# Moving the second chunk's state products, y and their VectorE steps behind the FFN work of their slot

## The reference, cut to what matters

```python
def step(h, inp):
    x_c, dt_c, B_c, C_c = inp
    lcs = jnp.cumsum(dt_c * A, axis=1)
    ...
    M = jnp.exp(jnp.where(mask, diff, -jnp.inf))
    G = jnp.einsum('blhn,bihn->bhli', C_c, B_c)
    intra = jnp.einsum('bhli,bihp->blhp', M * G, x_c)
    inter = jnp.einsum('blh,blhn,bhpn->blhp', jnp.exp(lcs), C_c, h)
    total_decay = jnp.exp(lcsT[:, :, -1])
    h_new = total_decay[:, :, None, None] * h + jnp.einsum('bhl,blhp,blhn->bhpn', M[:, :, -1, :], x_c, B_c)
    return (h_new, intra + inter)
...
y = y + x_h * D[None, None, :, None]
y = y * jax.nn.silu(z)
y = rmsnorm(y, w_norm_out)
...
sh = jax.nn.relu(jnp.einsum('bsd,ndf->bsnf', x, sw1) + sb1)
shared = (jnp.einsum('bsnf,nfo->bsno', sh, sw2) + sb2).sum(axis=2) / NS
rh = jax.nn.relu(jnp.einsum('bsd,edf->bsef', x, rw1) + rb1)
eo = jnp.einsum('bsef,efo->bseo', rh, rw2) + rb2
routed = (top two experts of four, weighted)
```

## Time and profile before

| | us |
|---|---|
| median of 3 runs | 567.0 (566.67 to 570.47) |
| profiled execution, its own time | 565.39 |
| span of its trace | 563.7 |

### The profile page before, as it was taken

One profiled execution on the slowest core, in us unless ns is written; L12 is line 12 of the kernel. 1 busy time (PEld: TensorE's weight loads), 2 busy tenths in 40 slices (PEclk: granted clock), 3 DMA queues, 4 the chain that ended last, 5 costly groups with the idle time before them and its releaser, 6 DMA issues.

```text
span 563.7 us, 11668 instructions
## 1 busy us (share of the span) xinstructions
PE 542.6 (96%) x3912; PEld 428.5 (76%) x3912; DVE 443.3 (79%) x1044; ACT 352.3 (63%) x760; POOL 173.2 (31%) x232
## 2 busy tenths in 40 slices
PE   8887989999999999999999999999999999999996
PEld 7665767878777777877787777778777787877774
DVE  5887878978889787878888788887888788775654
ACT  4894578637775478736786387745786377752442
POOL 3083505521162203620155201722045211532010
PEclk9998999999999999999999999999999999999999
DMA  7650017200570007500371005500162004600130
GB/s 207 196 141 9 1 55 182 74 1 1 160 169 1 2 6 218 107 1 0 100 192 34 0 0 165 160 0 0 39 208 78 0 0 142 169 1 1 32 68 19
DMA packets 37353, 41.41 MB, mean 73 GB/s; under 512 B 3482, under 2 KB 27716, under 8 KB 37316
## 3 DMA queue, kind: packets, MB, share of 16 engines
q1 hardware_dynamic: 36724, 40.80, 26.0%
q10 hardware_dynamic: 592, 0.15, 0.1%
HBM read 37.79 MB, written 3.15 MB: 73 GB/s over the span
## 4 chain that ended last, share of the span: by engine, by line
PE 59%; DVE 21%; ACT 8%; issue 7%; DMA 2%; POOL 2%; DVEq 0%; ACTq 0%; SPq 0%; POOLq 0%
PE bank L426 9%; PE bank L428 6%; PE bank L427 6%; PE bank L536 6%; PE bank L641 5%; PE bank L642 5%; PE bank L643 5%; DVE cv L1124 5%; DVE act_l L1275 4%; PE bank L548 3%; ACT act_h L873 3%; PE bank L564 2%; PE bank L522 2%; DVE dsum L1140 2%; DVE dtv L1138 2%
## 5 line engine op out<-in xcount | busy, mean ns | idle before, releaser
L1275 DVE SCALAR_TENSOR_TENSOR act_l<-bank,act_h 128x512 fp32r<-128x512 f32 x192 | 131.7, 687 | 51.5 <-ACT act_h L873 49.9
L873 ACT ACTIVATE act_h<-bank 128x512 fp32r<-128x512 f32 x192 | 114.7, 597 | 81.9 <-PE bank L428 78.1
L1501 POOL TENSOR_TENSOR late<-late 128x512 f32<-128x512 f32 x31 | 39.8, 1285 | 166.9 <-DVE late L1283 166.9
L426 PE MATMUL bank<-fTl,w1h 128*128 128x512 f32 x192 | 87.0, 453 | 2.0 <-DVE act_l L1275 0.7
L893 ACT ACTIVATE seg<-seg,lneg 128x128 f32<-128x128 f32 x256 | 81.3, 395 | 0.0
L641 PE MATMUL bank<-act_l,w2h 128*128 128x512 f32 x192 | 77.6, 404 | 1.5 <-DVE act_l L1275 1.5
L642 PE MATMUL bank<-act_h,w2l 128*128 128x512 f32 x192 | 76.0, 396 | 0.0
L428 PE MATMUL bank<-fTh,w1h 128*128 128x512 f32 x192 | 75.7, 394 | 0.0
L427 PE MATMUL bank<-fTh,w1l 128*128 128x512 f32 x192 | 75.5, 393 | 0.0
L643 PE MATMUL bank<-act_h,w2h 128*128 128x512 f32 x192 | 75.5, 393 | 0.0
L1488 POOL TENSOR_TENSOR xw<-xs,seg 128x128 f32<-128x128 f32 x48 | 20.2, 421 | 147.0 <-ACT seg L893 69.8
(11 more groups left out here) (177 smaller groups left out, 1057.9 us busy)
## 6 DMA issues: line engine op xcount, KB each, us to landing
seg<-lc_rows SPq DMA_DIRECT2D x32, 512.0 KB, 3.8
late<-gk_rows SPq DMA_DIRECT2D x8, 1024.0 KB, 9.0
grow<-lc_rows SPq DMA_DIRECT2D x48, 128.0 KB, 4.9
x_in<-L_attn_hidden_dram SPq DMA_DIRECT2D x8, 256.0 KB, 2.8
out_dram<-late SPq DMA_DIRECT2D x8, 256.0 KB, 5.3
late<-L_ffn_sw_dram SPq DMA_DIRECT2D x2, 512.0 KB, 6.3
late<-L_ffn_rw_dram SPq DMA_DIRECT2D x1, 1024.0 KB, 7.1
CT<-L_attn_w_in_proj_dram SPq DMA_DIRECT2D x1, 512.0 KB, 5.3
```

The source lines that it names most:

```text
L426: mm(dst, stat_h, mov_l, start=True, stop=False)
L873: nc.scalar.activation(act_h[:, b % RING, :], HID[b % 2][:], ACT.Relu).then_inc(act_h_ready, 1)
L1275: v_.scalar_tensor_tensor(act_l[:, r, :], HID[b % 2][:], 0.0, f(act_h[:, r, :]), ALU.max, ALU.subtract)\
```

## The change

Nothing is computed differently. For the passes with a scan and an FFN, `y_product` of chunk 1 is taken from the front of slot 17 and put behind `first` and `second` of that slot; VectorE's step 2 of chunk 1 is taken from the front of the slot and put behind `routed_out` and `act_low`. The opening keeps its order.

```diff
@@ TensorE, scan_part and body
                     if step == 2:
-                        y_product(s, c)
+                        if c != 1:
+                            y_product(s, c)
...
                     if old := block_at(i - LAG, prev, older):
                         second(*old)
+                    if s is not None and i == CHUNKS_FROM + 5:
+                        y_product(s, 1)
@@ VectorE, scan_part and body
-                if i >= CHUNKS_FROM:
+                if i >= CHUNKS_FROM and (i != CHUNKS_FROM + 5 or is_seq(s, 0)):
                     attend(s, *divmod(i - CHUNKS_FROM, 3))
...
                     if (new := block_at(i, prev, older)) and not (i == 0 and prev is not None):
                         act_low(*new)
+                    if s is not None and i == CHUNKS_FROM + 5:
+                        attend(s, 1, 2)
```

## The result

The changed kernel takes **573.86 us** (median of 4 runs, 571.09 to 575.33), the kernel before 566.84 beside it: a ratio of 1.0121, with a 95% interval of 1.0092 to 1.015. A second set of runs gave 574.01 against 566.40, ratio 1.0149 (1.0108 to 1.0189). It is slower by more than 1%, 0.5 us from the forecast of 573.4.

What follows compares the result with a forecast made beforehand. TensorE, busy 96% of the span, was taken as the bound. 5.2 us (sequences 1 to 6) plus 1.2 (sequence 7) gave 6.4 on the profiled 565.39, so 571.8; with the median 1.6 higher, 573.4. Range 566.8 to 577.0.

Steps and rivals of the forecast that it cites:

- Steps 1 to 3: Slots 17 and 18: FFN products start earlier, `y_product` and GpSimd's work later; `state_m` is 2.3 us late.
- Step 4: VectorE's `state_m` collides with GpSimd's first decay mask, is stretched and ends 0.27 us behind it.
- the other bound: Alternative in step 4: `state_m` unstretched at 0.41 to 0.42 us, all that follows 0.16 us earlier.
- Steps 5 and 6: Silu(z) product meets `CTe`, `hn` waits for `late`; chunk 2's `mg` 1.38 us late, TensorE stands 0.86 longer, 5.2 in all.
- Step 7: Chunk 3's growth rows are issued late, ScalarE waits 2.1 us; costs TensorE 1.2 us, in sequence 7 only.
- I take nothing: Step 7's late growth rows cost nothing in sequences 1 to 6, where TensorE is itself 0.86 us late.
- (a): Rival: `hn` gets the ports ahead of `late`, TensorE keeps 0.23 us per pass: 565.4 to 567, chance 0.17.
- (b): Rival: growth rows land later and decide in every sequence, 1.65 us more each, 11.6 in all: 585, chance 0.10.
- (c): Rival: the change does nothing measurable, losses of steps 6 and 7 lie in unseen waits: 567, chance 0.03.

Runs made afterwards that it cites:

- the added GpSimd instruction: Changed kernel plus one useless 128x512 TENSOR_TENSOR on GpSimd right behind the first `late` of a pass: 584.13 us, ratio 1.0333.
- the kernel with both edits: Changed kernel with `hn` at the front of slot 17 and a third growth-row buffer: 566.27 us, ratio 0.9984; again 566.51, ratio 1.0000.
- the third buffer: Growth rows of chunks 1, 2 and 3 in buffers of their own; as the only edit to the changed kernel: 572.33 us, ratio 1.0096.
- the kernel before with both edits: Kernel before, in its old order, with `hn` ahead of `routed_out` at the end of slot 17 and a third growth-row buffer: 576.68 us, ratio 1.0186.
- the kernel with VectorE's order alone: Only VectorE's part of the change, against the kernel before; `y_product` stays ahead of the FFN products: 589.87 us, ratio 1.0421.

## Why the prediction was right, step by step

**Steps 1 to 3** came out. Against the last product of `second(11)`, `y_product` starts 0.23 later (0.23 predicted), `routed_out` 0.69 (0.59), `state_m` 1.95 (1.85), GpSimd's first mask 1.67 (1.68) and `late` 4.66 (4.68). The 0.10 of `routed_out` is new: it waited for a DMA. More of that below.

**Step 4**, `state_m` under the mask: right in sequences 4 to 6, 0.58 to 0.72 us with the end 0.28 behind the mask (0.27 predicted). In sequence 3 it came later still, behind a longer wait for the DMA, and took 0.50 under the `xw` behind the mask. In sequences 1, 2 and 7 the order of the two was the other one. VectorE and GpSimd in sequence 1:

```profile
102.58 0.41 DVE L1171 TENSOR_TENSOR state_m<-state,grow 128x256 f32<-128x256 f32 x1
...
104.66 3.05 DVE L1103 TENSOR_SCALAR hn<-x_in,mv,rs 128x128 f32<-128x128 f32 x4
```

```profile
102.62 0.88 POOL L1497 TENSOR_SCALAR_AFFINE_SELECT seg<-seg 128x508 f32<-128x508 f32 x1
```

`state_m` began 0.04 ahead of the mask, took 0.41, and the mask was the one stretched, 0.88 for 0.64. So the one that starts first goes through, in both directions. The Trainium skill's page "SBUF — State Buffer" has it so in its section "Who interferes with whom", and this trace agrees, with the 0.41 and the 0.88. Which of them is first hangs here on 0.1 us of `routed_out`. The prediction had taken the 0.41 of the other bound for an absence of contention. It also misread its 16 rows: none stood beside a mask, but the first one (0.41 us from 38.52) ran wholly inside a GpSimd TENSOR_TENSOR of 128x8 (line 1430, 37.48 to 39.13) and was not stretched, so not every pair of this sort collides. The silu(z) product then came ahead of `CTe`, but `hn` behind it met `CTe` and `late` both and took 3.05. Chunk 2's weights came 0.82 later than before there too; the 0.16 that the other bound would have saved were not saved.

**Steps 5 and 6** carry the forecast, and hold: chunk 2's weights 0.81 later in sequence 5 against 0.86, and 0.80 to 0.85 in all of sequences 1 to 6. The first experiment that takes `late` from `hn` and the one that takes `hn` from `late` both remove this wait, and the added GpSimd instruction lengthens it by what it adds to `hn`. The six passes together lost 4.3 us, not 5.2, so this term was over-sized by 0.9: chunk 2 was 0.82 late on the mean of six instead of 0.86, and by chunk 3 another 0.07 to 0.08 was made up each time (7.66 us from chunk 2's weights to chunk 3's where it was 7.74; the kernel with both edits, where TensorE doesn't wait, has 7.75). Why the products behind a wait stand closer I did not look into.

**Step 7** had the right place and a size that varies. It gave 1.2 us to sequence 7; measured were 0.5 and 2.2 in two traces. The step that failed is the transfer left out of it. `routed_out` multiplies by the gating rows, a load of 1 MB for which it did not have to wait at its old place: in sequence 5 before, the load landed at 360.37 and `routed_out` started at 362.27. The change moves it 2 us ahead, into the landing (364.26, with `routed_out` at 364.29): waits in slot 17 of sequences 3 to 6, of 0.9 to 1.5 us, where there was none, and in five passes of the second trace, with 2.35 in its sequence 7. There the load landed 10.26 us behind its issue where it had been 8.60. No run moved this load, so its share is read from the traces alone. The prediction followed the growth rows, which are issued later, and not the rows that are needed sooner.

"I take nothing" for the growth rows in sequences 1 to 6 held, but only since TensorE was late already. With `hn` out of the way chunk 3's weights came up to 0.7 us later than before in a pass, and with the third buffer besides that was gone. Had the first term been smaller, this one would have come up in its place.

**The sum**: 6.4 us predicted. The two pairs of traces, from the opening's end, show 4.6 and 6.8, the medians 7.0 and 7.6. It is right within 0.5 us by cancelling: the passes' term was 0.9 too large, and what the medians hold beyond the traces stands in no term. Both traced executions of the changed kernel were the fastest of their sets (571.09 and 572.13), and 2 to 3 us lie between them and the medians. Part of it may be half-clock stretches: 5 of the 10 runs have a mean granted clock of 0.990 to 0.992 where the traced ones have 0.995. But one run with 0.995 took 578.86, so that isn't all; a later landing of the gating rows would do it too. No trace caught either, and the cause of these 2 to 3 us stays open.

**The rivals.** (a), `hn` ahead of `late`, did not occur in any of the twelve passes: GpSimd's waiting instruction went first each time. What it would have given is nearest to the two kernels that keep `hn` and `late` apart: 1.009 times the time of before, and no gain, since the growth rows then decide. The gain that (a) counted on shows only with these out of the way too: 0.2 us in most passes of the traces, as predicted, and nothing in the medians. (b) fell by its condition, as above. (c) fell.

## What to carry to other kernels

When instructions of one engine are moved, list for every instruction in the moved block both what it frees later and what it needs sooner: the second list held the transfer that I had not priced. Before moving VectorE work to where GpSimd works, lay the two engines' lists side by side and look for the place where one of them is idle; the same `hn` was stretched by nothing or by 1.0 to 2.7 us depending only on that. And when a removed cause gives back less than it cost, look for a second one right behind it before giving up the first: here each alone gave back about a third, both together everything.

## What the runs showed of the hardware

**A VectorE group beside GpSimd instructions back to back.** Four `hn` with one SBUF input took 1.10 us alone, 2.07 beside `late`, 2.08 beside `CTe`, 2.81 beside two GpSimd instructions, 3.05 meeting `CTe` and `late`, 3.80 meeting these two and the added one (sequence 2 of that kernel). VectorE got in for one of its own instructions between two of GpSimd's and then stood through the whole of the next, which was stretched in its turn, by 0.17 to 0.19 us (1.46 for 1.28). Between `state_m` and the mask it went by who was first even at 0.04 us, and the other was stretched.

**The granted clock after a wait.** In the kernel with the added instruction, TensorE stood 1.31 to 1.52 us ahead of chunk 2's `mg` products in each of six passes, which were otherwise alike. In two of them, with 1.46 and 1.49, 3.4 us at 1.2 GHz followed (granted clock 0.50), and chunk 3's weights came 1.6 us later than in the others. After waits of 1.31 to 1.37 us in six passes of the kernel before with both edits no such stretch is seen, nor after those of up to 0.8 in two traces of the changed kernel. In the kernel with VectorE's order alone, waits of 1.45 to 1.46 in sequences 3 to 6 were followed by such a stretch three times of four. What singles out the passes with such a stretch the traces don't show.

**Landing times.** The 128 KB growth rows of chunk 3 landed 3.1 us behind their issue in sequence 5, and 2.8 to 3.4 in the others, while the median over all such rows is 4.9. The 1 MB gating rows of sequence 7, issued at the same point of the program, landed after 8.60 us and in time in one execution, and after 10.26 us and 2.35 late for the same instruction in another.
